# Modulation of tiles 1 and 2 and tile 0's sum of squares as split fp32r products, with low parts in another order

## The chip, the cores and the metric

One core of one Trainium2 chip. The metric is the device time of one execution in microseconds (us), as the median of several runs. TensorE is called PE here, VectorE DVE, ScalarE ACT, GpSimd POOL.

## What is computed

The reference adds four layers to x (4 batches of 1024 tokens, 512 features), each to the result of the one before. The change touches the third:

```python
x = x + _L0_cond_ref(...)          # MLP with an expert part
x = x + _L1_cond_ref(...)          # one linear layer per subject
x = x + _L2_cond_ref(...)          # below
x = x + _L3_cond_ref(...)          # one linear layer per expert
...
ctx = causal_ema(x, tau_ctx)
wg = sigmoid(concat([x, ctx]) @ Wg.T + bg)
gated = x * wg
h1 = gelu(x @ Wn1.T + bn1)                       # 128 features
mod = 0.5 + sigmoid(h1 @ Wn2.T + bn2)            # 4 rates
traces = causal_ema(gated * mod[..., None], tau) # one for each rate
temporal = sum over rates of traces * softmax(blend)
gate = sigmoid(temporal @ Wtemp.T + btemp)
soma = gelu(x @ Wsoma.T + bsoma)
out = (soma * gate) @ Wout.T
mu, var = out.mean(-1), out.var(-1)
return (out - mu) / sqrt(var + 1e-05) * gamma + beta
```

## The kernel before

The 4096 tokens are 8 tiles of 512 (`NT = 8`, `LAST = 7`), the 512 features 4 chunks of 128 (`KC = 4`). Features lie on partitions. The first part of the program (layers 0 and 1) ends at about 780 us; the third and fourth layers run in rounds, round r working on tile r's gate and traces, on tile r-1's `te`, `ou` (temporal and output products) and sum of squares, and on tile r-2's last layer `l3`.

Every large product is done in split form: an operand is a high part (rounded to fp32r, an ACT copy) and a low part (operand minus high part, a DVE subtraction, `low_part`), and `split_product` issues three matmuls, hi*hi, hi*lo, lo*hi (L1610 to L1612). A few small products are plain float32.

Each engine has one queue of instructions, written out by hand and worked off in order; engines meet through counting semaphores (`on.wait_ge`). There is no planner. The names that matter:

- `n1(i)` on PE makes x @ Wn1 of tile i; `h1_of(i)` on ACT is its gelu; `h1_hi_of(i)` (ACT, L1178) and `h1_low(i)` (DVE, recorded at L2092 like every low part) split it; `mo(i)` on PE is h1 @ Wn2, plain for tiles 0 to 2 (L1767) and split for tiles 3 to 7 (L1763, recorded at L1610 to L1612 as `h_hi`, `h_lo`).
- `mod_of(i)`, `modulation_out(i)`, `modulation_back(i)` on ACT take the result through DRAM into `mod_t`, 4 rows broadcast to all partitions, which DVE's `drive_of` (L2329) multiplies in.
- `gate(i, m)` on PE is chunk m of the gate: 12 matmuls of 256 columns on the context (`Q`) and two halves of tokens of 12 such matmuls each (`gate_tokens`). `mo(i)` is issued inside `gate(i, 0)`: for tiles 1 and 2 between the first half of tokens and Q, for tiles 3 to 7 after Q.
- `q_of` (ACT) copies Q to `q_sb`, `gate_sum` (DVE, L2308) adds it, `wg_tanh` (ACT), `gated_of` (DVE, L2316).
- For each chunk DVE then does four rates d: `drive_of`, `trace_of` (a scan, L2340) and `add_of` (L2351), in the groups `traces_a` to `traces_d`; `traces_d` is the last scan and the last add. After the add, ACT's `temporal_hi(i, m)` (L1228) makes the high part of temporal, and DVE's `temporal_low(i, p)` the low parts of chunks p and p+1 in one instruction of 1024 columns. `te(i, m)` on PE needs both for chunks 0 and 1 before its first matmul, and those of chunks 2 and 3 from its seventh.
- `x1_hi`, `x1_lo`, `x2_of(LAST, m)`, `te_by_chunk` are the last steps of layers 0 and 1 and the first `te`. `te_by_chunk` waits before the product of chunk 0 and bank m for `x2_of(LAST, m)`.
- `sum_squares(i)` on DVE (L2405) adds the squares of tile i's output, `ss(i)` on PE sums over partitions with a matrix of ones: plain (L1934) for tiles 0, 6, 7, split (L1929, L1931) for 1 to 5, with `sumsq_hi` on ACT and `sumsq_low` on DVE.
- `wn2_hl` are the two parts of Wn2, zeroed by POOL (L1018), filled once by ACT (L1511) and DVE (L2693).

Of the kernel before, what the change touches and what calls it, by code (L numbers as in the profile page):

```python
# [15 lines left out]
TAUS = 4  # L16
# [27 lines left out]
def build(nc, x, tok16, tok8, small, fc1_w, fc2_w, exp_w, exp_b, l1_w, l1_b, wg, wn1, wsoma, wtemp, wout,  # L44
# [16 lines left out]
    with ctx:  # L61
# [448 lines left out]
        def mo_split_no(i):  # L510
            return max(0, i - 2)

        def ss_split_no(i):
            return min(i, LAST - 1 - 1)
# [437 lines left out]
        def _(eng):  # L952
# [58 lines left out]
            modulation_back(0)  # L1011
            last_columns(0, 0)
# [4 lines left out]
            on.wait_ge(s_made, len(MADE))  # L1017
            eng.memset(wn2_hl[:, :, :].bitcast(F32), 0.0).then_inc(s_wn2, 1)  # L1018
# [4 lines left out]
        def _(eng):  # L1023
# [151 lines left out]
            def h1_hi_of(i):  # L1175
                on.wait_ge(s_h1, i + 1)
                on.wait_ge(s_pe["SS"], i - 1)
                eng.activation(h1_hi[:, :], h1[:, :], ACT.Copy).then_inc(s_h1hi, 1)  # L1178
# [74 lines left out]
            def o_of(i, m):  # L1253
# [18 lines left out]
                if m == 0:  # L1272
                    if i:
                        on.wait_ge(s_pe["SS"], i)
                        on.wait_ge(s_pe["MO"], min(i + 2, NT))
                    eng.activation(sumsq[:, :], ps[:, :], ACT.Square).then_inc(s_sq, 1)
                else:
                    if i == LAST - 1:
                        on.wait_ge(s_pe["WG"], KC * NT)
                    eng.activation(square_of(i, m), ps[:, :], ACT.Square).then_inc(s_sq, 1)  # L1280
# [229 lines left out]
            on.wait_ge(s_wn2, 1)  # L1510
            eng.activation(wn2_hl[:, 0, 0:TAUS], wn2_sb, ACT.Copy).then_inc(s_wn2, 1)  # L1511
            soma_of(1, 0)
            soma_of(1, 1)
# [6 lines left out]
            for r in range(2, NT):  # L1520
                if r == 2:
                    h1_of(r)
                    temporal_hi(r - 1, 3)
                else:
                    temporal_hi(r - 1, 3)
                    h1_of(r)
                    h1_hi_of(r)
# [77 lines left out]
        def _(eng):  # L1605
# [151 lines left out]
            def mo(i):  # L1757
                if i > 2:

                    on.wait_ge(s_wn2, 3)  # L1760
                    on.wait_ge(s_h1hi, mo_split_no(i))
                    on.wait_ge(s_h1lo, mo_split_no(i))
                    split_product(mo_bank(i)[0:WN2, :], wn2_hl[:, 0, :], wn2_hl[:, 1, :], h1_hi[:, :], h1_lo[:, :],  # L1763
                                  True, True).then_inc(s_pe["MO"], 1)
                    return
                on.wait_ge(s_h1, i + 1)
                eng.matmul(mo_bank(i)[0:TAUS, :], wn2_sb, h1[:, :], start=True, stop=True  # L1767
                           ).then_inc(s_pe["MO"], 1)
# [4 lines left out]
            def gate(i, m):  # L1773
# [43 lines left out]
                if m == 0 and i:  # L1817
                    gate_tokens(i, m, 0, 1)
                    if i < 3:
                        mo(i)  # L1820
# [5 lines left out]
                if m == 0 and i > 2:  # L1826
                    mo(i)
# [92 lines left out]
            def ss(i):  # L1920
# [6 lines left out]
                if 0 < i < LAST - 1:  # L1927
# [160 lines left out]
        def _(eng):  # L2088
# [597 lines left out]
            traces_c(1, 2)  # L2686
# [147 lines left out]
```

## Time and profile before

| | |
|---|---|
| median of 3 runs | 1283.33 us (1283.28 to 1283.66) |
| the profiled execution's own time | 1283.78 us |
| its span in the profile | 1282.0 us |
| PE busy | 1270.6 us (99%) |
| PE weight loads | 1066.2 us (83%) |
| DVE busy | 1065.3 us (83%) |
| ACT busy | 720.7 us (56%) |
| POOL busy | 79.8 us (6%) |

The page cuts the span into 40 slices. PE's busy share is 9 tenths or more in all but the last, DVE's is so in most slices from the 23rd on. A matmul's record lasts longer than the distance to the next one's start, since matmuls overlap in the array: in a full queue one of 512 columns starts 0.227 us after the one before (one of 256 columns 0.12 us), while its record lasts 0.39 (0.28) us. The cost of an instruction to PE's queue is therefore read from start to start.

### The profile page before, as it was taken

The page shows a single profiled execution, that of the slowest core. Times are in us where ns is not written, and L with a number is a line of the kernel's source. Part 1 is how long each engine was busy: PE and PEld are TensorE (multiplying, and loading weights), DVE is VectorE, ACT ScalarE, POOL GpSimd, SP SyncE. Part 2 cuts the span into 40 slices and gives each one's busy share as a digit, 9 for nine tenths or more (in the row PEclk, how much of TensorE's full clock was granted, in tenths as well). Part 3 has the DMA queues.
Part 4 walks back from the last instruction along what each step waited for, and adds up shares of the span by engine and source line. Part 5 has one row for each costly group of instructions (what it writes and reads, how often), then busy time and mean ns, then how long its engine had stood idle before and what let it go on. Part 6 is the DMA issues. An engine that isn't in the chain of part 4 may idle for free. (4 is left out here: it accounts for less than half of the span.)

```text
span 1282.0 us, 17509 instructions
## 1 busy us (share of the span) xinstructions
PE 1270.6 (99%) x6109; PEld 1066.2 (83%) x6109; DVE 1065.3 (83%) x1682; ACT 720.7 (56%) x1369; POOL 79.8 (6%) x118
## 2 busy tenths in 40 slices
PE   9999999999999999999999999999999999999998
PEld 7788888888888888888888888888888888888876
DVE  7977777787786987786875998999999999998973
ACT  6577565776475875475764343453636363636344
POOL 0010000000000000000000211002000200020000
PEclk9999999999999999999999999999999999999999
DMA  8357553648745757644649887957466646663301
GB/s 294 101 171 235 187 180 132 221 157 262 222 156 159 242 171 259 202 157 156 231 153 347 316 333 256 394 188 254 157 246 230 237 175 228 240 223 139 131 17 66
DMA packets 115151, 263.68 MB, mean 206 GB/s; under 512 B 10440, under 2 KB 32968, under 8 KB 109944
## 3 DMA queue, kind: packets, MB, share of 16 engines
q1 hardware_dynamic: 95200, 184.32, 41.9%
q10 hardware_dynamic: 15032, 62.45, 13.8%
q0 software_dynamic: 4832, 15.79, 3.3%
q8 instruction: 49, 0.80, 0.3%
q14 instruction: 38, 0.31, 0.1%
HBM read 182.24 MB, written 80.28 MB: 205 GB/s over the span
## 5 line engine op out<-in xcount | busy, mean ns | idle before, releaser
L1610 PE MATMUL bank<-h_hl,w_hl 128*128 128x512 f32 x512 | 199.6, 390 | 0.0
L1611 PE MATMUL bank<-h_hl,w_hl 128*128 128x512 f32 x512 | 199.2, 389 | 0.0
L1612 PE MATMUL bank<-h_hl,w_hl 128*128 128x512 f32 x512 | 199.2, 389 | 0.0
L1610 PE MATMUL bank<-t_hi,sp_hl 128*128 128x512 f32 x448 | 175.3, 391 | 3.6 <-DVE t_lo L2092 1.1
L1611 PE MATMUL bank<-t_lo,sp_hl 128*128 128x512 f32 x448 | 174.4, 389 | 0.0
L1612 PE MATMUL bank<-t_hi,sp_hl 128*128 128x512 f32 x448 | 174.3, 389 | 0.0
L1610 PEld LDWEIGHTS bank<-h_hl,w_hl 128*128 128x128 f32 x512 | 96.1, 188 | 21.7 <-issue 1.8
L1612 PEld LDWEIGHTS bank<-h_hl,w_hl 128*128 128x128 f32 x512 | 96.1, 188 | 20.1
L1611 PEld LDWEIGHTS bank<-h_hl,w_hl 128*128 128x128 f32 x512 | 96.1, 188 | 19.6
L1610 PEld LDWEIGHTS bank<-t_hi,sp_hl 128*128 128x128 f32 x448 | 84.1, 188 | 24.4 <-issue 2.5
L1612 PEld LDWEIGHTS bank<-t_hi,sp_hl 128*128 128x128 f32 x448 | 84.1, 188 | 17.6
L1611 PEld LDWEIGHTS bank<-t_lo,sp_hl 128*128 128x128 f32 x448 | 84.1, 188 | 17.0
L2329 DVE SCALAR_TENSOR_TENSOR drive<-gated,small_sb,mod_t 128x512 f32<-128x512 f32 x128 | 92.5, 744 | 3.1 <-DVE gated L2316 0.3
L2092 DVE TENSOR_TENSOR w_hl<-w_raw,w_hl 128x512 fp32r<-128x512 f32 x128 | 86.5, 684 | 4.3 <-ACT w_hl L1064 3.9
L1131 ACT ACTIVATE h_hl<-hb_in 128x512 fp32r<-128x512 f32 x64 | 40.1, 627 | 83.9 <-DMA hb_in<-hb_dram 59.3
L1064 ACT ACTIVATE w_hl<-w_raw 128x512 fp32r<-128x512 f32 x128 | 78.3, 619 | 6.3 <-PE bank L1612 6.3
L2340 DVE TENSOR_TENSOR_SCAN drive<-alpha,trace_last,drive 128x512 f32<-128x512 f32 x64 | 80.2, 1274 | 0.5
L2340 DVE TENSOR_TENSOR_SCAN drive<-alpha,drive 128x512 f32<-128x512 f32 x64 | 76.3, 1213 | 0.4
L997 POOL COPY trace_last<-drive 128x1 f32<-128x1 f32 x64 | 48.2, 754 | 412.6 <-DVE drive L2340 411.3
L2092 DVE TENSOR_TENSOR h_hl<-hb_in,h_hl 128x512 fp32r<-128x512 f32 x64 | 43.8, 685 | 35.7 <-ACT h_hl L1131 35.7
L1048 ACT ACTIVATE sp_hl<-s_raw_sb 128x256 fp32r<-128x256 f32 x128 | 50.9, 412 | 38.5 <-PE bank L1612 37.0
L1611 PE MATMUL bank<-x_slot,wg_hl 128*128 128x256 f32 x256 | 72.4, 283 | 0.0
(232 smaller groups left out, 3080.1 us busy)
## 6 DMA issues: line engine op xcount, KB each, us to landing
wg_hl<-wg_dram ACTq DMA_DIRECT2D x24, 1536.0 KB, 8.4
fc_raw<-in_fc_w SPq DMA_DIRECT2D x32, 512.0 KB, 4.2
hb_dram<-hb_out SPq DMA_DIRECT2D x64, 256.0 KB, 2.2
hb_in<-hb_dram ACTq DMA_DIRECT2D x64, 256.0 KB, 4.4
x2hl_dram<-x_hl POOLq DMA_DIRECT2D x28, 512.0 KB, 5.5
x_slot<-x2hl_dram SPq DMA_DIRECT2D x26, 512.0 KB, 4.1
wg_hl<-wg_dram SPq DMA_DIRECT2D x8, 1536.0 KB, 8.8
stage<-in_l_w SPq DMA_DIRECT2D x32, 256.0 KB, 3.4
```

The lines of the kernel that those rows point to most:

```text
L997: eng.tensor_copy(trace_last[:, TAUS * c + d:TAUS * c + d + 1], traced[:, TOK - 1:TOK]).then_inc(s_tracel, 1)
L1048: eng.activation(sp_hl[n % RING][:, 0, :, :], product_source(n), ACT.Copy).then_inc(s_shi, 1)
L1064: eng.activation(w2_hl[v % 3][:, 0, :, :], w2_raw[:, j, :, :], ACT.Copy).then_inc(s_w2hi, 1)
L1131: eng.activation(h_hl[v % 4][:, 0, :], hb_in[v % 4][:, :], ACT.Copy).then_inc(s_hhi, 1)
L1610: eng.matmul(ps, w_hi, x_hi, start=first, stop=False, skip_group_check=resumed)
L1611: eng.matmul(ps, w_hi, x_lo, start=False, stop=False, skip_group_check=resumed)
L1612: return eng.matmul(ps, w_lo, x_hi, start=False, stop=final, skip_group_check=resumed)
L2092: return eng.tensor_tensor(lo, raw, hi.bitcast(F32), ALU.subtract)
L2329: eng.scalar_tensor_tensor(drive[d % 2][:, :], gated[:, :], blend_sb[:, TAUS * c + d:TAUS * c + d + 1], mod_t[:, d, :], ALU.mult, ALU.mult ...
L2340: eng.tensor_tensor_scan(traced, alpha[:, 1 + d:2 + d].to_broadcast([P, TOK]), traced, start, ALU.mult, ALU.add).then_inc(s_trace, 1)
```

## The change

`mo(1)` and `mo(2)` become split products and stand after Q as those of the later tiles do; `ss(0)` becomes a split product. `wn2_hl` is made earlier: POOL's memset right after tile 0's modulation, ACT's and DVE's copies at the end of round 0. ACT gets `h1_hi_of(1)`, `h1_hi_of(2)` and `sumsq_hi(0)`, DVE gets `h1_low(1)`, `h1_low(2)` and `sumsq_low(0)`. In all rounds `temporal_low(r, 0)` moves ahead of the last scan and add of chunk 3, `h1_low(r + 1)` stands ahead of `temporal_low(r, 2)` instead of behind it, and ACT does `h1_of` and `h1_hi_of` ahead of `temporal_hi(r - 1, 3)`.

```diff
         def mo_split_no(i):
-            return max(0, i - 2)
+            return i
         def ss_split_no(i):
-            return min(i, LAST - 1 - 1)
+            return i + 1
...
# POOL
             modulation_back(0)
+            on.wait_ge(s_made, len(MADE))
+            eng.memset(wn2_hl[:, :, :].bitcast(F32), 0.0).then_inc(s_wn2, 1)
             last_columns(0, 0)
...
-            on.wait_ge(s_made, len(MADE))
-            eng.memset(wn2_hl[:, :, :].bitcast(F32), 0.0).then_inc(s_wn2, 1)
...
# ACT
             def h1_hi_of(i):
                 on.wait_ge(s_h1, i + 1)
-                on.wait_ge(s_pe["SS"], i - 1)
+                if i > 1:
+                    on.wait_ge(s_pe["SS"], i - 1)
...
                 x1_hi(LAST, c)
+            on.wait_ge(s_wn2, 1)
+            eng.activation(wn2_hl[:, 0, 0:TAUS], wn2_sb, ACT.Copy).then_inc(s_wn2, 1)
             h1_of(1)
+            h1_hi_of(1)
             mod_of(1)
             modulation_out(1)
...
-            on.wait_ge(s_wn2, 1)
-            eng.activation(wn2_hl[:, 0, 0:TAUS], wn2_sb, ACT.Copy).then_inc(s_wn2, 1)
             soma_of(1, 0)
+            sumsq_hi(0)
             soma_of(1, 1)
...
             for r in range(2, NT):
-                if r == 2:
-                    h1_of(r)
-                    temporal_hi(r - 1, 3)
-                else:
-                    temporal_hi(r - 1, 3)
-                    h1_of(r)
-                    h1_hi_of(r)
+                h1_of(r)
+                h1_hi_of(r)
+                temporal_hi(r - 1, 3)
                 mod_of(r)
...
# PE
             def mo(i):
-                if i > 2:
-
+                if i:
                     on.wait_ge(s_wn2, 3)
...
                 if m == 0 and i:
                     gate_tokens(i, m, 0, 1)
-                    if i < 3:
-                        mo(i)
                 on.wait_ge(s_cslot, 16 * KC * (i + 1))
...
-                if m == 0 and i > 2:
+                if m == 0 and i:
                     mo(i)
...
-                if 0 < i < LAST - 1:
+                if i < LAST - 1:
                     on.wait_ge(s_ssqhi, ss_split_no(i))
...
# DVE
             traces_d(0, 3)
+            on.wait_ge(s_wn2, 2)
+            low_part(wn2_hl[:, 1, 0:TAUS], wn2_sb, wn2_hl[:, 0, 0:TAUS]).then_inc(s_wn2, 1)
+            h1_low(1)
             for c in range(KC):
                 x1_lo(LAST, c)
...
             sum_squares(0)
-            traces_c(1, 2)
+            trace_of(1, 2, 2)
+            sumsq_low(0)
+            drive_of(1, 2, 3)
+            add_of(1, 2, 2)
             traces_d(1, 2)
             traces_a(1, 3)
             traces_b(1, 3)
             traces_c(1, 3)
+            temporal_low(1, 0)
             traces_d(1, 3)
-            on.wait_ge(s_wn2, 2)
-            low_part(wn2_hl[:, 1, 0:TAUS], wn2_sb, wn2_hl[:, 0, 0:TAUS]).then_inc(s_wn2, 1)
-            temporal_low(1, 0)
+            h1_low(2)
             temporal_low(1, 2)
             for r in range(2, NT):
-                if r > 2:
-                    h1_low(r)
...
                 traces_c(r, 3)
+                temporal_low(r, 0)
                 traces_d(r, 3)
-                temporal_low(r, 0)
+                if r < LAST:
+                    h1_low(r + 1)
                 temporal_low(r, 2)
```

The other edits are one more condition each (`o_of` waits for `mo` of tile 1 also in tile 0).

How the rows stand on DVE at the end of round 0 (the scan and add of the last chunk, then `x1_lo`, the four `x_hl` rows, and `gate_sum(1, 0)`), before:

```order
L2340 SCALAR_TENSOR_TENSOR drive_107<-alpha,drive_107 128x512
L2351 TENSOR_TENSOR temporal<-drive_107,temporal 128x512
L2092 TENSOR_TENSOR x_hl<-x_raw_89,x_hl 128x512 x4
L2308 TENSOR_TENSOR bank<-bank,q_sb 128x512
L2092 TENSOR_TENSOR temporal_lo<-temporal,ts_hi 128x1024 x2
```

and in the change:

```order
L2336 SCALAR_TENSOR_TENSOR drive_107<-alpha,drive_107 128x512
L2347 TENSOR_TENSOR temporal<-drive_107,temporal 128x512
L2088 TENSOR_TENSOR wn_hl<-small_sb,wn_hl 128x4
L2088 TENSOR_TENSOR h_lo<-h_92,h_hi 128x512
L2088 TENSOR_TENSOR x_hl<-x_raw_89,x_hl 128x512 x4
L2304 TENSOR_TENSOR bank<-bank,q_sb 128x512
```

The low parts of Wn2 and of tile 1's h1 stand ahead of `x1_lo` now.

On DVE at the end of round 1, chunk 3 of tile 1 and the first work of round 2 (`o_sb` is `z_of`), before:

```order
L2340 SCALAR_TENSOR_TENSOR drive_106<-alpha,trace_last,drive_106 128x512
L2329 SCALAR_TENSOR_TENSOR drive_107<-gated,small_sb,mod_t 128x512
L2351 TENSOR_TENSOR temporal<-drive_106,temporal 128x512
L2340 SCALAR_TENSOR_TENSOR drive_107<-alpha,trace_last,drive_107 128x512
L2351 TENSOR_TENSOR temporal<-drive_107,temporal 128x512
L2092 TENSOR_TENSOR wn_hl<-small_sb,wn_hl 128x4
L2092 TENSOR_TENSOR temporal_lo<-temporal,ts_hi 128x1024 x2
L2415 SCALAR_TENSOR_TENSOR o_sb<-o_sb,small_sb,rstd 128x512 x4
```

and in the change:

```order
L2336 SCALAR_TENSOR_TENSOR drive_106<-alpha,trace_last,drive_106 128x512
L2325 SCALAR_TENSOR_TENSOR drive_107<-gated,small_sb,mod_t 128x512
L2347 TENSOR_TENSOR temporal<-drive_106,temporal 128x512
L2088 TENSOR_TENSOR temporal_lo<-temporal,ts_hi 128x1024
L2336 SCALAR_TENSOR_TENSOR drive_107<-alpha,trace_last,drive_107 128x512
L2347 TENSOR_TENSOR temporal<-drive_107,temporal 128x512
L2088 TENSOR_TENSOR h_lo<-h_92,h_hi 128x512
L2088 TENSOR_TENSOR temporal_lo<-temporal,ts_hi 128x1024
L2411 SCALAR_TENSOR_TENSOR o_sb<-o_sb,small_sb,rstd 128x512 x4
```

`temporal_low(1, 0)` stands ahead of the last scan and add, and h1's low part for `mo(2)` behind them.

On DVE at the end of round 7, where no h1 follows (`sumsq` is `sum_squares(6)`), before:

```order
L2351 TENSOR_TENSOR temporal<-drive_106,temporal 128x512
L2340 SCALAR_TENSOR_TENSOR drive_107<-alpha,trace_last,drive_107 128x512
L2351 TENSOR_TENSOR temporal<-drive_107,temporal 128x512
L2092 TENSOR_TENSOR temporal_lo<-temporal,ts_hi 128x1024 x2
L2405 TENSOR_TENSOR sumsq<-sq_late,sumsq 128x512 x3
```

and in the change:

```order
L2347 TENSOR_TENSOR temporal<-drive_106,temporal 128x512
L2088 TENSOR_TENSOR temporal_lo<-temporal,ts_hi 128x1024
L2336 SCALAR_TENSOR_TENSOR drive_107<-alpha,trace_last,drive_107 128x512
L2347 TENSOR_TENSOR temporal<-drive_107,temporal 128x512
L2088 TENSOR_TENSOR temporal_lo<-temporal,ts_hi 128x1024
L2401 TENSOR_TENSOR sumsq<-sq_late,sumsq 128x512 x3
```

The two low parts are apart, and nothing stands between the last add and the second of them.

## Rows read from the trace of the kernel before

**Rows 1.** Busy time in a stretch of round 4; columns in the row's head

```profile
core 0: us, PE busy (x) PEld busy (x) DVE busy (x) ACT busy (x) POOL busy (x), PEclk, DMA share, GB/s
976.00:1008.00 32.00, 32.00 (x187) 28.29 (x186) 30.80 (x39) 13.74 (x25) 4.30 (x6) 1.00 0.43 156
```

**Rows 2.** PE timeline (start, duration in us, instruction) around the plain `mo(2)`

```profile
844.20 0.28 PE L1612 MATMUL bank<-x_slot,wg_hl 128*128 128x256 f32 x1
844.40 1.02 PE L1767 MATMUL bank<-h,small_sb 128*4 128x512 f32 x2
...
845.58 0.28 PE L1611 MATMUL bank<-ctx_slot,wg_hl 128*128 128x256 f32 x1
```

**Rows 3.** PE timeline around the split `mo(3)`; idle and releaser in brackets

```profile
911.26 0.28 PE L1612 MATMUL bank<-ctx_slot,wg_hl 128*128 128x256 f32 x1
912.25 0.42 PE L1610 MATMUL bank<-h_hi,wn_hl 128*64 128x512 f32 x1 [0.71 <-DVE h_lo L2092]
...
912.74 0.40 PE L1612 MATMUL bank<-h_hi,wn_hl 128*64 128x512 f32 x1
```

**Rows 4.** PE timeline around the plain `ss(0)`

```profile
833.58 0.40 PE L1612 MATMUL bank<-x_slot,wsoma_hl 128*128 128x512 f32 x1
...
834.91 0.40 PE L1611 MATMUL bank<-x_slot,wsoma_hl 128*128 128x512 f32 x1
```

**Rows 5.** PE timeline: plain `mo(1)`, first `l1(LAST)`, bank 3 of `te_by_chunk`

```profile
778.20 0.28 PE L1612 MATMUL bank<-x_slot,wg_hl 128*128 128x256 f32 x1
778.77 1.02 PE L1767 MATMUL bank<-h,small_sb 128*4 128x512 f32 x2 [0.29 <-ACT h L1172]
...
782.70 0.40 PE L1610 MATMUL bank<-x_hl,l_hl 128*128 128x512 f32 x1
...
795.65 0.39 PE L1610 MATMUL bank<-ts_hi,wtemp_hl 128*128 128x512 f32 x1
```

**Rows 6.** ACT timeline: gelu of tile 1; gelu and high part of tile 4

```profile
778.02 0.70 ACT L1172 ACTIVATE h<-bank,small_sb 128x512 f32<-128x512 f32 x1
...
974.42 0.73 ACT L1172 ACTIVATE h<-bank,small_sb 128x512 f32<-128x512 f32 x1 [0.42 <-PE bank L1754]
975.19 0.63 ACT L1178 ACTIVATE h_hi<-h 128x512 fp32r<-128x512 f32 x1
```

**Rows 7.** DVE timeline: low part of tile 4's h1, then `z_of`

```profile
975.85 0.69 DVE L2092 TENSOR_TENSOR h_lo<-h,h_hi 128x512 fp32r<-128x512 f32 x1 [0.24 <-ACT h_hi L1178]
976.46 2.73 DVE L2415 SCALAR_TENSOR_TENSOR o_sb<-o_sb,small_sb,rstd 128x512 f32<-128x512 f32 x4
```

**Rows 8.** DVE timeline: `gate_sum(1, 0)` and `x2_of(LAST, 3)`

```profile
784.31 0.70 DVE L2308 TENSOR_TENSOR bank<-bank,q_sb 128x512 f32<-128x512 f32 x1 [2.59 <-ACT q_sb L1207]
...
794.13 0.72 DVE L2250 SCALAR_TENSOR_TENSOR x_raw<-bank,l_b_sb,x_raw 128x512 f32<-128x512 f32 x1
```

**Rows 9.** DVE timeline: last scan and last add of round 1

```profile
844.69 1.28 DVE L2340 TENSOR_TENSOR_SCAN drive<-alpha,trace_last,drive 128x512 f32<-128x512 f32 x1
846.00 0.69 DVE L2351 TENSOR_TENSOR temporal<-drive,temporal 128x512 f32<-128x512 f32 x1
```

**Rows 10.** PE timeline: end of `te(1)`, start of `gate(2, 1)`

```profile
859.02 0.39 PE L1612 MATMUL bank<-ts_hi,wtemp_hl 128*128 128x512 f32 x1
859.44 0.36 PE L1610 MATMUL bank<-ctx_slot,wg_hl 128*128 128x256 f32 x1
```

**Rows 11.** DVE timeline: first drive of round 7; low parts of temporal at its end

```profile
1179.59 1.42 DVE L2329 SCALAR_TENSOR_TENSOR drive<-gated,small_sb,mod_t 128x512 f32<-128x512 f32 x2 [0.27 <-DVE gated L2316]
...
1228.08 2.35 DVE L2092 TENSOR_TENSOR temporal_lo<-temporal,ts_hi 128x1024 fp32r<-128x1024 f32 x2
```

**Rows 12.** The chain of waits: second of these low parts (start, us)

```profile
1229.22 1.22 DVE temporal_lo L2092
```

**Rows 13.** PE timeline: before and in `te(7, 0)`, and `ss(6)`

```profile
1228.47 0.39 PE L1612 MATMUL bank<-x_hi,l3w_hl 128*128 128x512 f32 x1
1229.35 0.50 PE L1610 MATMUL bank<-ts_hi,wtemp_hl 128*128 128x512 f32 x1 [0.49 <-DVE temporal_lo L2092]
...
1232.68 1.12 PE L1934 MATMUL bank<-sumsq,ones 128*128 128x512 f32 x2 [0.27 <-DVE sumsq L2405]
```

More of the change, by code:

```diff
@@ L1274, in o_of @@
                         on.wait_ge(s_pe["SS"], i)
-                        on.wait_ge(s_pe["MO"], min(i + 2, NT))
+                    on.wait_ge(s_pe["MO"], min(i + 2, NT))
                     eng.activation(sumsq[:, :], ps[:, :], ACT.Square).then_inc(s_sq, 1)
```

## The prediction

> **What bounds the kernel.** I read the busy table by stretches first, then PE's timeline from start to start, then DVE's and ACT's at the places of the change, and the chain of waits at the end. In a middle round PE is busy in 32.00 us of 32.00, DVE in 30.80, at a granted clock of 1.00, the higher of the two levels [rows 1]: PE's queue sets the time, and DVE follows little more than 1 us of slack per half round behind. In PE's timeline from 690 us on I looked for every start that comes later than the queue's step (0.227 us for 512 columns, 0.12 for 256). Few exist, and they are the places of this change: the plain products, a wait of `mo(3)` for DVE [rows 3], one of `te(7, 0)` [rows 13]. So a PE instruction saved counts in full, and so does each us that PE waits for a new low part. What has to be asked is where DVE stands when PE comes to the products that are split now.
>
> **Plain against split.** From the last 256-column product before `mo(2)` to the second after it pass 845.58 - 844.20 = 1.38 us; without `mo` two steps, 0.24, so the plain product costs 1.14 [rows 2]. The split one starts its third matmul 0.49 after its first, so three take 0.49 + 0.23 = 0.72 [rows 3]: 0.42 saved. `ss(0)`: 834.91 - 833.58 = 1.33 for two steps of 0.227, so 0.88 [rows 4]; two split matmuls take 0.45; 0.43 saved.
> The Trainium skill, FP8 and Floating Point Precision, section TensorE Precision Notes, counts true FP32 as four passes through the array. By that, as an estimate, a plain product would cost 0.91 and each of the three would save some 0.2 less than by the rows, and the sum would be 0.4 us higher for the two on PE's path; the rows show more than four steps, and I go by them.
>
> **Tile 1.** `mo(1)` needs a chain now. ACT's gelu started at 778.02 [rows 6]; the Wn2 copy ahead of it takes 0.1. High part 0.75 later, low part on DVE 0.66 after that [rows 6, 7], at 779.53; it lasts 0.69 [rows 7], and PE starts up to 0.1 after a low part's end (one that began at 1228.08 and took 1.22 released PE at 1229.35, [rows 11 to 13]). So `mo(1)` can start at 780.32. PE comes there at 778.20 + 0.12 + 1.44 (12 steps of Q) = 779.76 and waits 0.6. It ends 0.9 after its start, at 781.2, against 778.77 + 1.02 = 779.79 before [rows 5]: the modulation is 1.45 later. The first `l1(LAST)` is hardly later: `mo` until 781.04, tokens 1.44, 782.48; `x1_lo`, which stands behind the new low part, ends at about the same time, so within 0.1 of the 782.70 of before [rows 5].
> But ACT does `mod_of(1)` and `modulation_out(1)` ahead of `temporal_hi` and `q_of(1, 0)`, and `gate_sum(1, 0)` on DVE already waited 2.59 for that copy [rows 8]. It moves by 1.45, and behind it in DVE's queue all up to `x2_of(LAST, 3)`, less 0.16 of a wait for PE that it takes up: 794.13 + 1.29 = 795.42, end 796.14 [rows 8]. `te_by_chunk` starts on it at 796.24; before, it did at 795.65 [rows 5]. **+0.59**, and DVE, which then waits for PE at the next add, is as late.
>
> **Tile 0's sum of squares.** **-0.43** on PE. `sumsq_low(0)` takes one step of DVE, 0.60 (975.85 to 976.46, [rows 7]), and comes just in time, some 0.2 ahead of PE. DVE is now 0.59 + 0.60 = 1.19 later than before.
>
> **Tile 2, the large term.** PE reaches `mo(2)` at 844.32 + 1.44 + 0.59 - 0.43 = 845.92 (844.32 is a step after 844.20, [rows 2]). On DVE the last add of round 1 stood at 846.00 [rows 9]. Add 1.19, add `temporal_low(1, 0)` ahead of it (step 1.14: two take 2.35, one 1.22, [rows 11, 12]): 848.33. A step of 0.60 later, 848.93, `h1_low(2)` starts, and ends at 849.62; PE starts at 849.72. **The wait is +3.80**. ACT is no cause: its high part needs `n1(2)` only, which PE ends before the first half of tokens. The product itself saves **-0.42**. Queued behind it on PE: the second half of tokens, and `te(1)`, for which all is ready.
> Two waits of before go in return. `gate(2, 1)` started 859.44 - 859.02 = 0.42 after its neighbour, 0.19 over a step, 0.08 more behind it [rows 10], since it waited for DVE; PE is 3.6 later now and DVE only 1.8: **-0.27**. `mo(3)`: 912.25 - 911.26 - 0.12 = **-0.87** [rows 3]: DVE is ahead of PE in round 2, `h1_low(3)` is no longer behind two `temporal_low`, and it is bound by `n1(3)` as in [rows 7], half a us ahead of PE.
>
> **Rounds 3 to 6.** `temporal_low(r, 2)` stands behind `h1_low(r + 1)`, which waits for PE's `n1`; so `z_of` starts 1.14 later against PE than before. That is taken up at `sum_squares`, where DVE waited for squares; PE's products on its work have 2 us or more in hand. I cost it at 0. If that cover were gone, up to 1.14 per round would show at `ss`.
>
> **The end.** In round 7 DVE has no such wait until the end. It starts 1.14 later, takes up the 0.27 ahead of the first drive [rows 11], and stays 0.87 late against PE. Before, `temporal_low(7, 0)` started at 1228.08 and PE's `te(7, 0)` followed at 1229.35, against 1228.70 if nothing had held it [rows 11, 13]. Now that low part stands a scan and an add earlier (1.31 + 0.60, [rows 9, 7]): 1228.08 - 1.91 + 0.87 = 1227.04, end 1228.26: no wait. But the add comes at 1229.49, ends at 1230.18, the high part on ACT follows (0.66) and `temporal_low(7, 2)` starts at 1230.86, where it was 1229.22 [rows 12]; before, the first low part covered ACT's copy. PE wants it at 1228.70 + 6 x 0.227 = 1230.06 and gets it at 1232.2, a wait of 2.2. `sum_squares(6)` follows, 1.64 later, and `ss(6)`, which DVE already held back [rows 13], too. **+1.64**; I take the chain through DVE, since both waits are in it.
>
> **The sum.** 0.59 - 0.43 + 3.80 - 0.42 - 0.27 - 0.87 + 1.64 = 4.04, +4.0 us. The profiled execution took 1283.78 with a span of 1282.0; the span becomes 1286.0, that execution's time 1287.8, and since the median of the runs is 0.45 below the profiled one, the median becomes 1283.33 + 4.04 = **1287.4**.
> Bounds of what no row shows: tile 1's chain 0 to 1.1 (its PE slack fully covering, or the full shift less 0.35 of waits); `mo(2)`'s wait 3.2 to 4.4 (one DVE step less or more); the end -0.76 (only the old wait goes) to 2.2; rounds 3 to 6 from 0 to 1.1.
>
> **Rivals.**
> 1. The end is covered: DVE arrives so early against PE in round 7 that `temporal_low(7, 2)` costs nothing, and PE keeps the 3.3 us by which it is late as a lead for DVE. For it: DVE waits in the middle rounds. Against it: each round fixes DVE to PE again through `n1` and `h1_low`. 4.0 - 1.6 = 2.4: 1285.7, just within 0.2%.
> 2. PE's late time is given back, since DVE's chain leads at the end. Against it: PE is full in rounds 3 to 6 [rows 1]. Half of the wait, 1.9 us, back: 1285.5.
> 3. Faster: `h1_low(2)` is there when PE comes. It decides at 845.92 against 849.62: DVE would have to be 3.7 us ahead of where its rows put it. Then 0 or little for tile 1, -0.43, -0.42, -0.87 and -0.76: -2.5, 1280.8. Only if a DVE queue were not worked off in order could it be.
> 4. The granted clock falls to its lower level in the pause at `mo(2)`, the longest of PE after the start; no pause of this trace is nearly so long, and the clock is 1.00 in the stretches read [rows 1]. If it stayed low for as long as the pause, half of 3.8 would be lost on top: 1289.3.
> The Trainium skill, TensorE: Matmul & The Clock Gate, section What's actually happening, has the clock halved after an idle window; no run here shows it.
> 5. The change does not do what it says: excluded by the order of rows above.
>
> **Chances.** The forecast 0.70; rival 1 0.12, rival 2 0.07, rival 3 0.04, rival 4 0.07. A measurement of this kernel can tell 0.2%, 2.6 us, from no change. Slower by more: 0.70 + 0.07, and a small part of rivals 1 and 2, 0.79. Within: 0.17. Faster: 0.04. The range takes in rivals 1 and 2, and the upper bounds of tile 1's chain and the wait: 1285.3 to 1289.0.
>
> **What would show it.** In the changed profile: a wait of PE for `h_lo` of 3 to 4 us near 846 us, in round 2 and nowhere else of that size; 0.5 us or so at the split `mo(1)` and at `te_by_chunk`; no wait at `mo(3)`; then PE full until `te(7, 0)`, which stops before its seventh matmul for `temporal_lo` for 2 us. It would be wrong if the wait at `mo(2)` is under 1.5 us, if new waits stand in every round, or if the clock is below 1.00 after 850 us.

## The result and the profile after

| | before | after |
|---|---|---|
| median of the runs that were compared (six of each) | 1283.3 us (1282.84 to 1283.66) | 1289.15 us (1287.98 to 1289.6) |
| ratio to the kernel before | | 1.0042, 95% interval 1.0032 to 1.0052 |
| the profiled execution's own time | 1283.78 us | 1287.98 us |
| its span | 1282.0 us | 1286.2 us |
| PE busy | 1270.6 us | 1270.4 us |
| DVE busy | 1065.3 us | 1067.7 us |

The change is slower, by 0.42%. The forecast was 1287.4 (1285.3 to 1289.0); the median is 1.75 us above it and 0.15 above the range. By the ratio and the 1283.33 of the prediction the time is 1288.7, inside the range. The profiled execution, with 1287.98, was the fastest of the six. Direction and place were right, and one term, the granted clock, was missing from the sum.

The part of the program ahead of `gate(1, 0)`, which the change hardly touches, differs from execution to execution: the first matmul of `gate(1, 0)` starts at 776.89 in the profile before, at 776.54 after, and between 776.21 and 777.47 in the thirteen profiles of this document. Below, lengths are therefore taken from that matmul to the start of the last one of the program. PE's timeline of the profile after, first and last row of that length (start, duration, instruction; idle time and releaser in brackets):

```profile
776.54 0.28 PE L1609 MATMUL bank<-x_slot,wg_hl 128*128 128x256 f32 x1
...
1281.86 0.39 PE L1611 MATMUL bank<-ts_hi,l3w_last 128*128 128x512 f32 x1
```

This length is 505.32 us; before it was 1276.98 - 776.89 = 500.09. So +5.23 in PE's queue. The two spans differ by less, 4.2: the change's profile is 0.35 shorter ahead of this length, and 0.7 behind it, where 1286.2 - 1281.86 = 4.3 us pass from the start of the last matmul to the end of the span, against 1282.0 - 1276.98 = 5.0 before. Behind the last matmul come ACT's last copies and the stores of the output. That part is 4.3 in all nine profiles of kernels whose `ss(0)` is split, and 4.7 to 5.1 in the four where it is plain; why, no run shows, and the prediction has no term for it.

The length divides as follows (starts of the first matmuls of `te(1)`, `te(2)`, `te(6)` and `ss(6)` in both timelines; the last column is made of the terms of the prediction):

| stretch | before | after | difference | forecast |
|---|---|---|---|---|
| `gate(1, 0)` to `te(1)` | 71.45 | 76.28 | +4.83 | +3.54 |
| `te(1)` to `te(2)` | 66.07 | 64.74 | -1.33 | -1.14 |
| `te(2)` to `te(6)` | 259.10 | 259.07 | -0.03 | 0 |
| `te(6)` to `ss(6)` | 59.17 | 60.96 | +1.79 | +1.64 |
| `ss(6)` to the last matmul | 44.30 | 44.27 | -0.03 | 0 |

Only the first row misses by more than 0.2 us. PE's timeline there, at `mo(2)` (it answers to [rows 2]):

```profile
845.39 0.28 PE L1611 MATMUL bank<-ctx_slot,wg_hl 128*128 128x256 f32 x1
849.35 0.66 PE L1609 MATMUL bank<-h_hi,wn_hl 128*64 128x512 f32 x1 [3.68 <-DVE h_lo L2088]
849.81 0.63 PE L1610 MATMUL bank<-h_lo,wn_hl 128*64 128x512 f32 x1
850.23 0.63 PE L1611 MATMUL bank<-h_hi,wn_hl 128*64 128x512 f32 x1
850.66 0.41 PE L1609 MATMUL bank<-x_slot,wg_hl 128*128 128x256 f32 x1
850.87 0.41 PE L1610 MATMUL bank<-x_slot,wg_hl 128*128 128x256 f32 x1
...
852.70 0.28 PE L1611 MATMUL bank<-x_slot,wg_hl 128*128 128x256 f32 x1
852.82 0.40 PE L1609 MATMUL bank<-ts_hi,wtemp_hl 128*128 128x512 f32 x1
```

The wait is there: 849.35 - 845.39 - 0.12 = 3.84, forecast 3.80. But behind it the matmuls do not follow at 0.227 and 0.12 us: they follow at 0.46, 0.42, 0.43, and then at 0.21, until 852.3. The busy table by stretches (columns in its head) says why:

```profile
core 0: us, PE busy (x) PEld busy (x) DVE busy (x) ACT busy (x) POOL busy (x), PEclk, DMA share, GB/s
845.00:849.00 4.00, 0.67 (x6) 0.47 (x4) 3.97 (x5) 0.37 (x1) 0.00 (x0) 0.98 0.03 11
849.00:852.00 3.00, 2.65 (x10) 2.18 (x11) 2.84 (x5) 1.33 (x3) 0.00 (x0) 0.50 0.00 0
852.00:856.00 4.00, 4.00 (x22) 3.45 (x21) 3.89 (x6) 2.08 (x5) 0.00 (x0) 0.96 0.05 19
```

The granted clock is 0.50, the lower of its two levels (1.2 instead of 2.4 GHz), from 849 to 852; in the trace the stretch begins at 848.88, inside the pause, and lasts 3.41 us. A matmul that starts in it costs up to twice its step: from `mo(2)`'s first matmul to `te(1)`'s pass 852.82 - 849.35 = 3.47 us, where 3 steps of 0.227 and 12 of 0.12 would be 2.12, so 1.35 us more (1.34 by the starts one by one; a run below, in which the clock stays up, gives 1.30). That is the missing term: 3.54 + 1.34 = 4.88 against 4.83. It is the mechanism of rival 4. The Trainium skill, TensorE: Matmul & The Clock Gate, section What's actually happening, has the clock halved after an idle window; this trace agrees, with 0.50 behind a pause of 3.68 us.

DVE's timeline ahead of it (answers to [rows 9]) shows who was late:

```profile
844.86 0.69 DVE L2347 TENSOR_TENSOR temporal<-drive,temporal 128x512 f32<-128x512 f32 x1
845.46 1.22 DVE L2088 TENSOR_TENSOR temporal_lo<-temporal,ts_hi 128x1024 fp32r<-128x1024 f32 x1
846.59 1.28 DVE L2336 TENSOR_TENSOR_SCAN drive<-alpha,trace_last,drive 128x512 f32<-128x512 f32 x1
847.91 0.69 DVE L2347 TENSOR_TENSOR temporal<-drive,temporal 128x512 f32<-128x512 f32 x1
848.52 0.68 DVE L2088 TENSOR_TENSOR h_lo<-h,h_hi 128x512 fp32r<-128x512 f32 x1
849.36 1.23 DVE L2088 TENSOR_TENSOR temporal_lo<-temporal,ts_hi 128x1024 fp32r<-128x1024 f32 x1 [0.16 <-ACT ts_hi L1229]
```

No gap stands ahead of `h_lo`: DVE works without a break up to it, and `temporal_low(1, 0)`, the last scan and the last add lie between PE's arrival and its start.

The smaller places, PE's and DVE's rows. Tile 1 (answers to [rows 5, 8]): `mo(1)` waits 0.31, the first `l1(LAST)` is not later, `gate_sum` waits 3.48 instead of 2.59, and bank 3 of `te_by_chunk` waits 0.26 for `x2_of(LAST, 3)`:

```profile
779.88 0.42 PE L1609 MATMUL bank<-h_hi,wn_hl 128*64 128x512 f32 x1 [0.31 <-DVE h_lo L2088]
...
782.20 0.50 PE L1609 MATMUL bank<-x_hl,l_hl 128*128 128x512 f32 x1
...
795.68 0.50 PE L1609 MATMUL bank<-ts_hi,wtemp_hl 128*128 128x512 f32 x1 [0.26 <-DVE x_raw L2246]
```

and on DVE:

```profile
785.62 0.70 DVE L2304 TENSOR_TENSOR bank<-bank,q_sb 128x512 f32<-128x512 f32 x1 [3.48 <-ACT q_sb L1208]
...
794.90 0.73 DVE L2246 SCALAR_TENSOR_TENSOR x_raw<-bank,l_b_sb,x_raw 128x512 f32<-128x512 f32 x1
```

From `gate(1, 0)` to that matmul pass 795.68 - 776.54 = 19.14 us, before 18.76: +0.38 (forecast +0.59). `ss(0)` (answers to [rows 4]) and `mo(3)` (to [rows 3]) start at PE's step, without a wait:

```profile
833.75 0.40 PE L1611 MATMUL bank<-x_slot,wsoma_hl 128*128 128x512 f32 x1
833.98 0.39 PE L1925 MATMUL bank<-ts_hi,ones 128*128 128x512 f32 x1
834.21 0.40 PE L1927 MATMUL bank<-sumsq_lo,ones 128*128 128x512 f32 x1
834.45 0.40 PE L1609 MATMUL bank<-x_slot,wsoma_hl 128*128 128x512 f32 x1
...
915.32 0.28 PE L1611 MATMUL bank<-ctx_slot,wg_hl 128*128 128x256 f32 x1
915.44 0.39 PE L1609 MATMUL bank<-h_hi,wn_hl 128*64 128x512 f32 x1
```

The end (answers to [rows 11 to 13]), in PE's timeline:

```profile
1231.59 0.39 PE L1611 MATMUL bank<-x_hi,l3w_hl 128*128 128x512 f32 x1
1231.82 0.39 PE L1609 MATMUL bank<-ts_hi,wtemp_hl 128*128 128x512 f32 x1
...
1235.40 0.50 PE L1609 MATMUL bank<-ts_hi,wtemp_hl 128*128 128x512 f32 x1 [2.06 <-DVE temporal_lo L2088]
...
1237.59 1.13 PE L1930 MATMUL bank<-sumsq,ones 128*128 128x512 f32 x2 [0.54 <-DVE sumsq L2401]
```

and in DVE's:

```profile
1230.21 1.22 DVE L2088 TENSOR_TENSOR temporal_lo<-temporal,ts_hi 128x1024 fp32r<-128x1024 f32 x1
1231.35 1.28 DVE L2336 TENSOR_TENSOR_SCAN drive<-alpha,trace_last,drive 128x512 f32<-128x512 f32 x1
1232.66 0.69 DVE L2347 TENSOR_TENSOR temporal<-drive,temporal 128x512 f32<-128x512 f32 x1
1234.12 1.23 DVE L2088 TENSOR_TENSOR temporal_lo<-temporal,ts_hi 128x1024 fp32r<-128x1024 f32 x1 [0.77 <-ACT ts_hi L1229]
```

`te(7, 0)` starts at once and stops before its seventh matmul; the 0.77 is ACT's copy, which nothing covers any more.

### The profile page after: what moved, and what is told of

Same layout as the page of the kernel before. It is cut to its first block, busy times and chain, and to the rows that moved or that the text cites. A ratio compares the mean times of both kernels' runs of the same rounds, so it can differ in the third digit from the quotient of the medians.

```text
span 1286.2 us, 17521 instructions
## 1 busy us (share of the span) xinstructions
PE 1270.4 (99%) x6111; PEld 1068.1 (83%) x6111; DVE 1067.7 (83%) x1685; ACT 722.5 (56%) x1372; POOL 79.8 (6%) x118
## 4 chain that ended last, share of the span: by engine, by line
PE 83%; DVE 11%; ACT 2%; issue 2%; DMA 2%; POOL 0%; ACTq 0%; DVEq 0%
PE bank L1609 28%; PE bank L1611 27%; PE bank L1610 27%; DVE drive L2336 3%; DVE drive L2325 1%; DVE temporal L2347 1%; DMA mod_t<-mod_dram 1%; DMA hb_in<-hb_dram 1%; DVE w_hl L2088 1%; DVE t_lo L2088 0%; DVE h_hl L2088 0%; DMA x_raw<-in_x 0%; DVE gated L2312 0%; DVE x_raw L2240 0%; DVE sumsq L2401 0%
## 5 line engine op out<-in xcount | busy, mean ns | idle before, releaser
L1610 PE MATMUL bank<-x_slot,wg_hl 128*128 128x256 f32 x256 | 72.8, 284 | 0.0
L1609 PE MATMUL bank<-x_slot,wg_hl 128*128 128x256 f32 x256 | 72.8, 284 | 0.0
```

The source lines that it names most:

```text
L1609: eng.matmul(ps, w_hi, x_hi, start=first, stop=False, skip_group_check=resumed)
L1610: eng.matmul(ps, w_hi, x_lo, start=False, stop=False, skip_group_check=resumed)
```

## Experiments

Eleven kernels. "Length" is the one from `gate(1, 0)` to the last matmul in its profile; "clock" says whether the trace has a stretch at 0.50 inside that length. In an execution's mean clock one such stretch of 3.41 us shows as 0.999 (3.41 x 0.5 / 1286 = 0.0013) and two as 0.997; a low stretch behind the last product shows too, by itself as 0.999 (as in a_mo2_plain), so the mean clock alone does not count the falls exactly.

| kernel | time, us (range) | ratio, 95% interval | length | clock |
|---|---|---|---|---|
| before | 1283.0 to 1283.3 | 1 | 500.09 | 1.00 |
| the change | 1289.15 (1287.98 to 1289.6) | 1.0032 to 1.0052 | 505.32 | low at 848.88 |
| a_mo2_plain | 1285.75 (1285.12 to 1286.92) | 1.001 to 1.0028 | 503.04 | 1.00 |
| a_mo2_early | 1287.93 (1286.31 to 1288.3) | 1.002 to 1.0045 | 504.62 | low at 853.84 |
| a_tail_old | 1287.87 (1287.25 to 1288.45) | 1.0024 to 1.0051 | 504.65 | low at 849.1 |
| a_fill | 1288.37 (1286.59 to 1290.6) | 1.0028 to 1.0056 | 504.78 | low at 1235.28 |
| a_mo1_plain | 1288.06 (1287.59 to 1289.09) | 1.0026 to 1.0053 | 504.84 | low at 849.43 |
| b_h1_r2 | 1282.96 (1282.2 to 1283.32) | 0.9987 to 1.0005 | 499.57 | 1.00 |
| b_low_order | 1284.32 (1283.68 to 1285.5) | 0.9999 to 1.0017 | 500.43 | 1.00 |
| b_ss_only | 1283.48 (1282.91 to 1284.23) | 0.9991 to 1.0009 | 501.02 | 1.00 |
| a_fill2 | 1287.94 (1287.45 to 1289.01) | 1.0021 to 1.0048 | 504.87 | 1.00 |
| best1 | 1285.35 (1284.6 to 1287.26) | 1.0006 to 1.0024 | 502.07 | 1.00 |
| b_best2 | 1282.23 (1281.78 to 1283.51) | 0.9981 to 0.9999 | 498.83 | 1.00 |

### The wait at mo(2)

**mo(2) plain again**, in its old place, without `h1_hi_of(2)` and `h1_low(2)`:

```diff
                 if m == 0 and i:
                     gate_tokens(i, m, 0, 1)
+                    if i in (2,):
+                        mo(i)
...
-                if m == 0 and i:
+                if m == 0 and i and i not in (2,):
                     mo(i)
...
-            h1_low(2)
             temporal_low(1, 2)
```

> The change with mo(2) plain and in its old place, without h1_hi(2) and h1_low(2); tile 1's modulation and tile 0's sum of squares stay split, low parts stay in the new order. Theory A: no wait at mo(2), no slow clock; DVE is one step (0.6, sumsq_low(0)) late at gate(2, 1), which waits 1 to 1.5 us; mo(3) does not wait: +0.6 - 0.9 + 1.8 at the end = +1.5: 1284.8 (1284.3 to 1285.3). Rival B (the loss is in the new order of low parts in all rounds, not in tile 2): 1287 or more.

1285.75, about 3.4 us less than the change; by the lengths it is 2.28 less, and some 1.3 of that is the clock's. The time is above what was expected because DVE's lateness shows elsewhere: the seventh matmul of `te(1, 0)` waits 1.00 us for `temporal_lo`, and `gate(2, 1)` waits 0.74 at 861.99. So mo(2)'s 3.68 us was not all its own; what it hides of DVE's lateness behind it, 1.7 us, is paid anyway as soon as PE is on time.

**h1_low(2) earlier on DVE**, ahead of the last drive, scan and adds of chunk 3:

```diff
-            traces_c(1, 3)
+            trace_of(1, 3, 2)
+            h1_low(2)
+            drive_of(1, 3, 3)
+            add_of(1, 3, 2)
             temporal_low(1, 0)
             traces_d(1, 3)
-            h1_low(2)
             temporal_low(1, 2)
```

> The change with h1_low(2) on DVE ahead of the last drive of chunk 3 in round 1 (right after the scan of rate 2) instead of behind the last add; same instructions. Theory A (DVE's queue is full in rounds 1 and 2, so that its three added steps show somewhere): PE has no wait at mo(2) and no slow clock, but it meets DVE again at gate(2, 1), which waits some 2 us for the first spikes of tile 1 (0.19 us before); sum against before +1.5 there, -0.9 at mo(3), +1.8 at the end: 1285.8 (1285.3 to 1286.3). Rival B (only the place of h1_low(2) cost time, DVE had room): wait gone without another, 4.8 less than the change: 1284.4 or below.

No wait at `mo(2)`, and 1.2 us gained in the median, with overlapping ranges (0.70 by the lengths). The pause stands behind it now, in PE's timeline:

```profile
852.40 0.50 PE L1609 MATMUL bank<-ts_hi,wtemp_hl 128*128 128x512 f32 x1 [2.15 <-DVE temporal_lo L2088]
```

and the clock falls again, in the busy table by stretches (columns as above):

```profile
852.00:853.50 1.50, 1.10 (x5) 0.93 (x6) 1.50 (x3) 0.34 (x1) 0.00 (x0) 1.00 0.02 5
853.50:857.50 4.00, 4.00 (x12) 3.14 (x11) 4.00 (x7) 1.49 (x3) 0.00 (x0) 0.57 0.02 7
```

The work on DVE decides, and its order says mainly at which product PE pays. The place was `te(1, 0)`, and not `gate(2, 1)` as the first theory had it, and the slow clock that it had ruled out came.

### The end

**Both `temporal_low` of round 7 behind the last add**, as before the change:

```diff
-                temporal_low(r, 0)
+                if r < LAST:
+                    temporal_low(r, 0)
                 traces_d(r, 3)
                 if r < LAST:
                     h1_low(r + 1)
+                else:
+                    temporal_low(r, 0)
                 temporal_low(r, 2)
```

> The change with both temporal_low of round 7 behind the last add again, as before; the other rounds as in the change. Theory A (in the new order ACT's copy of chunk 3 stands uncovered on DVE's chain, 0.77 us in the profile; the other 0.9 of the end come from DVE being later against PE since z_of moved behind h1_low): te(7, 0) waits 1.3 us before its first matmul instead of 2.1 before its seventh, ss(6) comes 0.8 earlier; 0.8 less than the change: 1288.3 at the median, 1287.2 in its fastest runs. Rival B (all of the end's 1.8 is the order there): 1.8 less, 1287.3 and 1286.2.

Length -0.67, median -1.3; `te(7, 0)` waits 1.37 once, at its first matmul, and `ss(6)` 0.32, instead of 2.06 and 0.54. From `te(6)` to `ss(6)` pass 60.05 us, against 60.96 in the change and 59.17 before: the order at the end is worth 0.91 of the 1.79 there (`te(1)` to `te(2)` takes 0.21 back in this profile). The rest goes with DVE being later against PE there: in this same order `te(7, 0)` waited 0.49 before the change [rows 13] and waits 1.37 here. That this too is the new order's, in the rounds before, and not the added work's, is shown by the run with the order alone below: it has no new work and is 1.55 us longer in this stretch.

### Tile 1 and tile 0's sum of squares

**mo(1) plain again**, in its old place, without `h1_hi_of(1)` and `h1_low(1)` (the edit has the form of the first one).

> The change, with mo(1) plain and in its old place; h1_hi_of(1) and h1_low(1) are gone. Theory A (each step of DVE behind tile 1's chain is handed on to h1_low(2)): the bank of te_by_chunk that waited 0.26 us for x_raw starts about 0.5 earlier, DVE is ahead by the same up to round 2, the wait at mo(2) stays at 3.6 to 3.7, and the time is 0.5 to 0.6 below the change's: 1288.6, or 1287.5 in an execution whose clock stays at 1.00. Theory B (the shift was taken up in DVE's own waits before te_by_chunk): no difference beyond PE's 0.42 for the plain product, so 1289.1 to 1289.6.

Length -0.48, median -1.1 with overlapping ranges; no wait at `te_by_chunk`, and still 3.67 at `mo(2)`, as the first theory has it. The clock falls here too, 0.40 us after `mo(2)` has begun (849.43 against 849.03).

**ss(0) alone**, on the kernel before: the split product, `sumsq_hi(0)` and `sumsq_low(0)`, with the change's condition at `o_of`.

```diff
             sum_squares(0)
-            traces_c(1, 2)
+            trace_of(1, 2, 2)
+            sumsq_low(0)
+            drive_of(1, 2, 3)
+            add_of(1, 2, 2)
```

> The kernel before with ss(0) split and nothing else: sumsq_hi(0) on ACT, sumsq_low(0) on DVE. Theory A (DVE decides the next two waits): PE gains 0.43 at ss(0) and loses it and DVE's step of 0.60 again at gate(2, 1), whose wait grows from 0.2 to about 1.2: 0.6 slower than before there, and what of it reaches mo(3) stays, 1283.6. Theory B (a PE instruction saved counts): 0.43 faster, 1282.6, gate(2, 1) as before.

The gain of 0.4 at `ss(0)` is there, and three waits take more than it gives. PE's timeline:

```profile
848.69 0.47 PE L1611 MATMUL bank<-ts_hi,wtemp_hl 128*128 128x512 f32 x1 [0.57 <-DVE temporal_lo L2093]
...
860.35 0.36 PE L1611 MATMUL bank<-ctx_slot,wg_hl 128*128 128x256 f32 x1 [0.52 <-DVE soma L2393]
...
913.17 0.42 PE L1611 MATMUL bank<-h_hi,wn_hl 128*64 128x512 f32 x1 [0.86 <-DVE h_lo L2093]
```

None, 0.19 and 0.71 stood there before. The length is 0.93 longer, of which 0.3 lies at `te_by_chunk`, ahead of the edit; behind the last matmul this profile is 0.7 shorter, as the change's is. The median is 0.2 higher, which the interval does not tell from none. A gain it is not.

### The order of low parts alone

**In all rounds**, on the kernel before, every product as before; `h1_low(r)` at the start of a round is gone, and ACT does `h1_of` and `h1_hi_of` ahead of `temporal_hi(r - 1, 3)`:

```diff
+                temporal_low(r, 0)
                 traces_d(r, 3)
-                temporal_low(r, 0)
+                if 1 < r < LAST:
+                    h1_low(r + 1)
                 temporal_low(r, 2)
```

> The kernel before with the new order of low parts in rounds 2 to 7 (round 7: temporal_low(7, 0) ahead of the last scan and add), every product as before. Theory A (the parts add up): -0.87 at mo(3) and +1.8 at te(7, 0) and ss(6): 1284.0, with a wait of 1.8 to 2.1 before the seventh matmul of te(7, 0) and none at its first. Theory B (the loss at the end comes only when DVE is as late as the changed kernel has it): the waits at te(7, 0) and ss(6) stay near 0.5 and 0.3, 1282.2.

1284.32 and a length of +0.34. `mo(3)` doesn't wait, and the end does, though DVE has no new work here:

```profile
1230.72 0.50 PE L1614 MATMUL bank<-ts_hi,wtemp_hl 128*128 128x512 f32 x1 [1.82 <-DVE temporal_lo L2096]
...
1232.92 1.12 PE L1938 MATMUL bank<-sumsq,ones 128*128 128x512 f32 x2 [0.52 <-DVE sumsq L2409]
```

That is the prediction's pair -0.87 and +1.64 alone, 0.8 by the sum. The rows have -1.04 (`te(1)` to `te(2)`) and +1.55 (`te(6)` to `ss(6)`), the medians +1.0. So nearly all of the end's cost is the price of the order, whatever work DVE has on top.

**In round 2 only** (`h1_low(3)` and its two ACT instructions):

```diff
-                if r > 2:
+                if r > 2 and not (r == 3):
                     h1_low(r)
...
                 temporal_low(r, 0)
+                if r == 2:
+                    h1_low(r + 1)
                 temporal_low(r, 2)
```

> The kernel before, with one piece of the new order, in round 2 alone: h1_low(3) ahead of temporal_low(2, 2) on DVE, h1_of(3) and h1_hi_of(3) ahead of temporal_hi(2, 3) on ACT. Theory A (mo(3)'s 0.87 us of waiting was for this order alone): no wait at mo(3), 0.8 to 0.9 less than before, 1282.2. Theory B (mo(3) did not wait in the changed kernel because its PE was 3 us late there): h_lo still ends after PE has come, the wait shrinks by 0.3 at most, 1282.8 to 1283.1.

No wait at `mo(3)`, but `mo(4)`, which had none, waits for its low part:

```profile
975.77 0.41 PE L1614 MATMUL bank<-h_hi,wn_hl 128*64 128x512 f32 x1 [0.26 <-DVE h_lo L2096]
```

0.42 of the 0.87 comes back one round later; length -0.52, median -0.33, within the interval. Neither theory's number, and the first one's place.

### The clock

**Idle matmuls ahead of mo(2)**, 15 of 512 columns, which compute nothing that is used:

```diff
+                if m == 0 and i == 2:
+                    on.wait_ge(s_wn2, 3)
+                    on.wait_ge(s_h1hi, mo_split_no(i))
+                    for _ in range(15):
+                        eng.matmul(mo_bank(i)[:, :], wn1_hl[:, 0, 0, :], x2_slot[x2_at(i, 0)][:, 0, :],
+                                   start=True, stop=True)
                 if m == 0 and i:
                     mo(i)
```

> The change, with 15 idle matmuls (512 columns, into the bank that mo(2) then overwrites) on PE between Q and mo(2), so that PE works through the 3.7 us in which it waits for h1_low(2); nothing else moves. Theory A (wait and clock): mo(2) starts at the same time, set by DVE, but the granted clock never leaves 1.00 after it; the half-speed stretch of the changed kernel's profile (3.4 us, 1.3 us lost) and the spread of its runs (1288.0 to 1289.6) go: 1287.4 +- 0.4, spread under 0.7. Rival B (the clock is not driven by the pause, or costs nothing in the end): 1288 to 1289.6 as before, half-speed records still there.

The clock stays at 1.00 at `mo(2)`:

```profile
849.95 0.45 PE L1609 MATMUL bank<-h_hi,wn_hl 128*64 128x512 f32 x1 [0.15 <-DVE h_lo L2094]
...
852.12 0.40 PE L1609 MATMUL bank<-ts_hi,wtemp_hl 128*128 128x512 f32 x1
```

From `mo(2)` to `te(1)` pass 2.17 us, where the change needed 3.47: the same instructions behind the same low part cost 1.30 less when the clock holds. The time is not what was expected, since the clock falls the pause of 1.80 us in `te(7, 0)` instead, 0.7 us after PE's work has gone on (PE's timeline; 0.227 would be the step):

```profile
1234.54 0.50 PE L1609 MATMUL bank<-ts_hi,wtemp_hl 128*128 128x512 f32 x1 [1.80 <-DVE temporal_lo L2094]
1234.88 0.40 PE L1610 MATMUL bank<-temporal_lo,wtemp_hl 128*128 128x512 f32 x1
1235.12 0.49 PE L1611 MATMUL bank<-ts_hi,wtemp_hl 128*128 128x512 f32 x1
1235.41 0.63 PE L1609 MATMUL bank<-ts_hi,wtemp_hl 128*128 128x512 f32 x1
1235.84 0.63 PE L1610 MATMUL bank<-temporal_lo,wtemp_hl 128*128 128x512 f32 x1
```

The five executions sort by their mean clock: 1.000 took 1286.59, 0.999 took 1288.07 to 1288.55, 0.997 took 1290.6. With the early `h1_low(2)` those at 1.000 took 1286.31 and 1286.4 and those below it 1287.8 to 1288.3, but there 0.997 took no longer than 0.999. So executions with a fall are 1.4 to 2 us longer here, and behind pauses of some 2 us it comes in some executions only. The change itself had no execution at 1.000, and its six do not sort: 0.999 took 1287.98, 1288.05, 1289.0 and 1289.46, 0.997 took 1289.3 and 1289.6. Something besides the clock, which no trace was taken of, separates them.

**Both pauses filled**, with 8 more idle matmuls ahead of the seventh of `te(7, 0)`:

```diff
             def te_part(i, m, c):
+                if i == LAST and m == 0 and c == 2:
+                    on.wait_ge(s_soma, KC * LAST + 2)
+                    for _ in range(8):
+                        eng.matmul(ss_bank(LAST - 1)[:, :], wtemp_hl[:, 0, 0, 0:P], ts_hi[:, 0, :],
+                                   start=True, stop=True)
```

> The change with idle matmuls in both of PE's pauses: 15 of 512 columns ahead of mo(2), 8 ahead of the seventh matmul of te(7, 0), each set just long enough to cover the wait; nothing is computed from them. Theory A (what the fill of mo(2) alone did not give was a second fall of the clock behind the pause at te(7, 0)): the granted clock is 1.00 from 690 us to the end of the products, mo(2) and te(7, 0) start where the low parts allow, as in the change, and the time is 1286.4 to 1286.8 with a spread under 0.8. Theory B (the half clock is not what separates 1287.9 from 1289.5): 1288 to 1289 with the change's spread.

The clock is 1.00 over the whole length, and the time is not what was expected: 1287.94, the three executions at 1.000 between 1287.45 and 1287.94. In the profiled one a part of the answer shows. ACT's queue, in round 7:

```profile
1178.60 1.90 ACTq L1198 DMA_DIRECT2D mod_t<-mod_dram  x2
1180.55 0.38 ACT L1207 ACTIVATE q_sb<-bank 128x256 f32<-128x256 f32 x1 [1.38 <-issue]
```

Issuing the transfer of the modulation took 1.90 us, where it took 0.81 in the profile of the change; `q_sb` and with it DVE's `gate_sum(7, 0)` came 1.09 later against `te(6)`, and DVE keeps 0.8 of it to the end, where `te(7, 0)` waits for it: from `te(6)` to `ss(6)` pass 61.76 us, 0.80 more than in the change. Without that the length would be 504.07, and 505.32 less 1.30 is 504.02. Whether the other executions had the same was not seen: that the fill at both places gives all of the clock's cost back is not shown.

### Together

**The change with its parts taken back:** mo(1) plain, the early `h1_low(2)`, the old end.

> The change with three of its parts taken back or moved: mo(1) plain in its old place, h1_low(2) ahead of the last scan and add of chunk 3 in round 1, both temporal_low of round 7 behind the last add. If the parts add up, from 1287.9 of the run with the early h1_low(2): -0.6 for mo(1), -0.9 for the end: 1286.4, and 1285 in an execution whose clock stays at 1.00. Rival: with mo(1) plain DVE is early enough at te(1, 0) that its pause is under 1.6 us and the clock doesn't fall: 1285.0 median. In neither case below the kernel before.

1285.35. Singly the three took 0.48, 0.70 and 0.67 off the length, 1.85 together; here it is 3.25 shorter. The 1.4 between is about the clock's price, for the clock stayed at 1.00: `te(1, 0)` waited 2.15 us in this profile without a fall. The rival's 1285.0 is near, but not by its mechanism: it had the pause under 1.6 us. The kernel is still slower than the one before: PE waits 2.15 us at `te(1, 0)`, 0.53 at `gate(2, 1)` and 1.13 at `te(7, 0)`, each time for DVE, which has `sumsq_low(0)` and `h1_low(2)` more to do.

**The kernel before with two edits:** that of round 2 above, and `ss(6)` one product later.

```diff
             te(LAST, 0)
+            te(LAST, 1)
             ss(LAST - 1)
-            for m in range(1, KC):
+            for m in range(2, KC):
                 te(LAST, m)
```

> The kernel before with two edits: h1_low(3) ahead of temporal_low(2, 2) as in the run before, and ss(6) behind te(7, 1) instead of behind te(7, 0). Theory A: te(7, 1) follows te(7, 0) at once, the 0.43 us by which ss(6) started late for DVE's sumsq goes, and so does 0.33 to 0.44 at mo(3): 1282.5, 0.8 less than before. Rival: ACT, whose rstd stands ahead of the gate of te(7, 1), is 1.5 later there and hands it on to spikes_low and ou(7, 0): 1283.3 or more.

1282.23 against 1283.21 of its neighbours, ratio 0.999 (0.9981 to 0.9999), length -1.26. `ss(6)` starts at PE's step:

```profile
1234.05 0.40 PE L1616 MATMUL bank<-ts_hi,wtemp_hl 128*128 128x512 f32 x1
1234.28 1.02 PE L1938 MATMUL bank<-sumsq,ones 128*128 128x512 f32 x2
```

It is the fastest kernel here, 1 us below the one before; that is less than the 0.2% (2.6 us) that the prediction calls measurable, and its interval just leaves out no change.

## Why the prediction was right, and where not

- **What bounds it:** right. PE's queue carries the time, and every difference inside the length was found as a start later than the step.
- **Tile 1's chain, +0.59:** mechanism and place right, 0.38 in the profile and 0.48 by the run with `mo(1)` plain. `mo(1)` waited 0.31 instead of 0.6.
- **The plain products' price:** the estimate from four passes, 0.91, is below the row of `mo(2)` (1.14) but above that of `ss(0)` (0.88). So "each of the three would save some 0.2 less" and "the rows show more than four steps" hold for `mo` and not for `ss(0)`; the sum does not use them.
- **ss(0), -0.43:** 0.40 on PE. Its price on DVE, 0.60, was carried into the next term, and that was needed: alone it gives nothing.
- **mo(2), +3.80:** 3.84. The product's -0.42, `gate(2, 1)` -0.27 and `mo(3)` -0.87 are in the table's first two rows, which fit within 0.2 once the clock is counted.
- **Rounds 3 to 6 at 0:** -0.03; nothing showed at `ss`, as forecast.
- **The end, +1.64:** 1.79, and 1.49 to 1.55 in four other kernels with the new order, with the wait before the seventh matmul (forecast 2.2, excess 2.22) and none at the first.
- **The step that failed** is the one that kept the clock at 1.00: "no pause of this trace is nearly so long, and the clock is 1.00 in the stretches read" was taken as a reason for a chance of 0.07, though it says only that the trace had no case to read. A pause of 3.7 us does lower it, in the profile of the change for 3.41 us at a cost of 1.34, and pauses of 1.80 and 2.15 us did too in some executions. The prediction's own sign of being wrong, a clock below 1.00 after 850 us, stood in the profile: it was 0.50 until 852.3.
- **What stays open:** with the clock the sum is 5.4, the 0.7 behind the last matmul takes it to 4.7, and the time would be 1288.0. The profiled execution took as much, and its nearness to the 1287.8 forecast for it is partly luck: the missing 1.34 was offset by 1.06 us outside the length, which the prediction did not have either. The median is 1.1 us higher. A second fall of the clock can be in two of the six executions, by their mean clock of 0.997; in two others, 1289.0 and 1289.46 at 0.999, the clock does not explain it. No trace of a slower execution was kept.
- **Rivals 1 to 3** did not happen: the end waits, nothing was given back in rounds 3 to 6, and `h1_low(2)` was late. Rival 4 came true on top of the forecast. That its 1289.3 is so near to 1289.15 is luck in part: it had put 1.9 us on the fall, which cost 1.3, and 1.1 us of the median has no known place.

## What to carry to other kernels

An exact product that is replaced by two or three fast ones moves work to the engines that make the parts: count the queue of that engine at the product, not only the product. Here the maker of the parts had about 1 us of slack: the 0.4 us saved on PE was lost at the next waits, and reordering its queue mostly moved the place. A pause of the main engine costs more than its length if the clock falls behind it; a forecast that creates a pause longer than any in the trace should give that fall its own term.

## What the runs showed of the hardware

- The granted clock fell to 0.50 for 3.41 us at each of the three unfilled pauses of 3.67 to 3.68 us (the change, a_tail_old, a_mo1_plain), beginning inside the pause in two and 0.40 us after it in one. It also fell behind pauses of 2.15 us (a_mo2_early) and 1.80 us (a_fill), beginning 1.4 and 0.7 us after PE had gone on. Six other pauses of 1.76 to 2.15 us had no fall (2.15 in best1, 2.06 in the change, 1.82 in b_low_order, 1.76 in three kernels), so a pause of this length does not decide it alone.
- Idle matmuls in the pause kept the clock at 1.00 there. They took no time from the product behind them (`mo(2)` began 72.73 us after `gate(1, 0)`, in the change 72.81).
- Issuing the same two transfers on ACT's queue took 0.81 us in most rounds of all profiles and 1.17 to 2.13 in single ones (1.17 in the kernel before, 1.45 in b_ss_only, 2.13 in a_fill). In the one read above DVE had no slack behind it, and handed it on to the end.
